# Gated delta rule in a two-layer decoder: whole 128x128 weights at the 32 and 64 levels of the block inverse, and the 64-row inverse turned from its kept transpose

## The chip, the cores and the metric

The kernel runs on one core of one Trainium2 chip. The metric is the device time of one execution in microseconds. Before the change three runs gave 4811.43, 4815.2 and 4816.7 us; the median is 4815.2 us. All work is float32 but for a few masks.

## The reference, cut to what matters

The whole program is two pre-norm decoder layers (attention, cross attention and a mixture of experts in each) on x of shape 8 x 256 x 256. The change touches one of the six parts only, the first part of the second layer:

```python
# x: (8, 256, 256); 16 key heads, DK = 128, values of 2 x 128 for each key head
q = causal_conv_silu(x @ Wq, qcw, qcb);  q = l2norm(q)
k = causal_conv_silu(x @ Wk, kcw, kcb);  k = l2norm(k)
v = causal_conv_silu(x @ Wv, vcw, vcb)
alpha, beta = sigmoid(x @ Wa), sigmoid(x @ Wb)
def step(state, inp):                       # for each of the 256 tokens of a sequence
    qt, kt, vt, at, bt = inp
    state = state * at
    err = vt - einsum('bhkv,bhk->bhv', state, kt)
    state = state + bt * einsum('bhk,bhv->bhkv', kt, err)
    return state, einsum('bhkv,bhk->bhv', state, qt)
out = outs.reshape(b, t, 32 * 128) @ Wo
```

## The kernel before, in words

The recurrence is not run token by token. For one head and one sequence (a *unit*; there are 16 x 8 = 128) the 256 tokens are two blocks of 128. Inside a block the errors solve a triangular system whose matrix is I plus the masked, decayed products of keys; its inverse, multiplied with the values, gives all errors at once. The inverse of a 128x128 block is built in levels. GpSimd inverts the four 32x32 diagonal blocks of each of the two blocks, for eight units at a time (lines 1285 to 1306). TensorE then joins them: at the 32 level two neighbouring inverses of 32 rows give one of 64 rows (`grow_off32`, `grow_t64`), at the 64 level two of 64 rows give the whole one (`grow_off64`, `grow_tt128`). `tt` holds the transpose of the inverse, which the solves need as weights; `t64` holds the upper 64-row inverse not transposed, which the 64 level needs as its moving operand. Before the change `t64` comes from a product of its own in `grow_t64` (line 1416).

The work is a software pipeline. In stage s the unit s is *projected* (8 matmuls with `wkqv`, line 1360), unit s-1 is *prepared* (convolution and silu on VectorE and ScalarE, lengths at 1395, products at 1371, v times Wo at 1385, scaled products into `lp` on VectorE at 1670 and 1673), unit s-16 is *grown* (the levels above) and unit s-17 is *given* (solves at 1447, 1453, 1459, outputs at 1467 to 1471, added to x on VectorE at 1710). There are 145 stages: 16 without a grown unit, 112 with all of them, and a tail of 17. Units alternate between two sets of buffers and PSUM banks (`h` = 0 and 1).

Each engine runs its part of a stage in a fixed written order (the functions named `stage`), and semaphores join them; an engine that comes to a wait holds all that it has behind it. On TensorE the order of a stage is in `stage` below. On ScalarE it is: keep w (1574), scale v (1557), tanh of part 0 (1534), keep tt64 (1564), keep the second w (1574), square (1540), the taps (1526), tanh of part 1, decay (1546), keep tt128 (1569), taps. On VectorE: convolve (1630), keep off32 (1682), convolve, rest (1702), convolve, silu (1640), keep t64 (1690), convolve, keep off64 (1695), keep lengths (1646), silu, add out (1710), scales (1655 to 1660), scale products (1670, 1673), convolve. So the square of the keys, which the lengths on TensorE wait for, stands on ScalarE behind the copy that waits for `solve_second`.

A float32 matmul is two instructions on TensorE (each a weight load and a matmul), so the trace has x4 where the code has two calls; a transpose is one.

Of the kernel before, what the change touches and what calls it, by code (L numbers as in the profile page):

```python
# [25 lines left out]
ALU = mybir.AluOpType  # L26
# [4 lines left out]
P = 128  # L31
B, S, D = 8, 256, 256
# [11 lines left out]
HALF = HD // 2  # L44
# [990 lines left out]
def delta_attention(k):  # L1035


    nc, ins = k.nc, k.ins
# [31 lines left out]
    t_ready = k.sems("dl_t_ready")  # L1070
    t_kept = k.sems("dl_t_kept")
    tt_ready = k.sems("dl_tt_ready")
    tt_kept = k.sems("dl_tt_kept")
# [20 lines left out]
    with ExitStack() as st:  # L1094
        def sb(name, shape, dt=F32):
            return k.sb(f"dl_{name}", shape, dt, st)
# [36 lines left out]
        diag = [sb(f"diag{h}", [P, 2, P]) for h in range(2)]  # L1133
        diag_t = [sb(f"diag_t{h}", [P, 2, HALF]) for h in range(2)]
        off32 = [sb(f"off32{h}", [P, 2, P]) for h in range(2)]
        off64 = [sb(f"off64{h}", [P, 2, HALF]) for h in range(2)]
        t64 = [sb(f"t64{h}", [HALF, 2, HALF]) for h in range(2)]
        tt = [sb(f"tt{h}", [P, 2, P]) for h in range(2)]
        wv = [sb(f"wv{h}", [P, 2, D]) for h in range(2)]
        rest = [sb(f"rest{h}", [P, D]) for h in range(2)]  # L1140
# [1 line left out]
        def bank(h, i, a, b, p0=0, p1=P):  # L1142
            return k.ps[h][p0:p1, i, a:b]

        def blocks(ap):
            return ap.rearrange("p (b s) -> p b s", b=2)
# [17 lines left out]
        with nc.Block() as block:  # L1164
# [93 lines left out]
            def _(pool):  # L1258

                for h in range(2):  # L1260
                    nc.gpsimd.memset(diag[h][:, :, :], 0.0)
                    nc.gpsimd.memset(diag_t[h][:, :, :], 0.0)
                    last = nc.gpsimd.tensor_copy(off32[h][:, :, :], k.ident[:, :].unsqueeze(1).to_broadcast([P, 2, P]))
                last.then_inc(made, 1)
                pool.wait_ge(loaded, 16 * 5)
# [66 lines left out]
            def _(pe):  # L1332
# [20 lines left out]
                def project_part(u, m):  # L1353
                    h = u.h
                    if m == 0:
                        pe.wait_ge(w_loaded[h], u.pair * 16 + 16)

                        wait_past(pe, lp_ready[h], u.count(1))
                    for c in range(DC):
                        last = nc.tensor.matmul(bank(h, m // 2, (m % 2) * S, (m % 2 + 1) * S),  # L1360
                                                wkqv[h][:, c, m * P:(m + 1) * P],
                                                k.xnT[:, c, u.seq * S:(u.seq + 1) * S],
                                                start=c == 0, stop=c == DC - 1)
                    if m % 2:
                        last.then_inc(projected[h], 1)
# [42 lines left out]
                                                diag_t[h][:, blk, :], start=True, stop=True)  # L1408
                    last.then_inc(off_ready[h], 1)

                def grow_t64(u):

                    h = u.h
                    pe.wait_ge(off_kept[h], u.count(2, 1))
                    for blk in range(2):
                        last = nc.tensor.matmul(bank(h, 2, P + blk * HALF, P + (blk + 1) * HALF, 0, HALF), diag[h][0:HALF, blk, 0:HALF],
                                                off32[h][0:HALF, blk, 0:HALF], start=True, stop=True)
                    last.then_inc(t_ready[h], 1)

                    pe.wait_ge(v_scaled[h], min(u.count(1, B), B * HK // 2) if u.fixed else u.count(1, B))  # L1420
                    for blk in range(2):
                        last = nc.tensor.matmul(bank(h, 3, blk * P, (blk + 1) * P), off32[h][:, blk, :],
                                                diag[h][:, blk, :], start=True, stop=True)
                    last.then_inc(tt_ready[h], 1)

                def grow_off64(u):
                    h = u.h
                    pe.wait_ge(t_kept[h], u.count(1, 1))
                    for blk in range(2):
                        last = nc.tensor.matmul(bank(h, 2, blk * HALF, (blk + 1) * HALF, 0, HALF),  # L1430
                                                lp[h][0:HALF, u.seq, blk * S + HALF:blk * S + P],
                                                t64[h][:, blk, :], start=True, stop=True)
                    last.then_inc(off_ready[h], 1)

                def grow_tt128(u):
                    h = u.h
                    pe.wait_ge(off_kept[h], u.count(2, 2))
                    pe.wait_ge(tt_kept[h], u.count(2, 1))
                    for blk in range(2):
                        last = nc.tensor.matmul(bank(h, 2, P + blk * HALF, P + (blk + 1) * HALF, 0, HALF), off64[h][HALF:P, blk, :],  # L1440
                                                tt[h][HALF:P, blk, HALF:P], start=True, stop=True)
                    last.then_inc(tt_ready[h], 1)

                def solve_first(u):
# [29 lines left out]
                def stage(j, s, project, prepared, turned, grown, given):  # L1474
                    if given is not None:
                        solve_first(given)
                    if grown is not None:
                        grow_off32(grown)
                    if project is not None:
                        project_part(project, 0)  # L1480
                    if given is not None:
                        solve_cross(given)
                    if grown is not None:
                        grow_t64(grown)
                    if project is not None:
                        project_part(project, 1)
                    if given is not None:
                        solve_second(given)
                    if project is not None:
                        project_part(project, 2)  # L1490
                    if grown is not None:
                        grow_off64(grown)
                    if prepared is not None:
                        lengths_of(prepared)
                        products_of(prepared, 0)
                    if given is not None:
                        mix(given)
                    if grown is not None:
                        grow_tt128(grown)
                    if project is not None:  # L1500
                        project_part(project, 3)
                    if prepared is not None:
                        products_of(prepared, 1)
                        give_v(prepared)
# [97 lines left out]
            def _(dve):  # L1602
# [84 lines left out]
                def keep_t64(u):  # L1687
                    h = u.h
                    dve.wait_ge(t_ready[h], u.count(1, 1))
                    nc.vector.tensor_copy(t64[h][:, :, :], blocks(bank(h, 2, P, S, 0, HALF))).then_inc(t_kept[h], 1)  # L1690

                def keep_off64(u):
                    h = u.h
                    dve.wait_ge(off_ready[h], u.count(2, 2))
                    nc.vector.tensor_scalar(off64[h][HALF:P, :, :], blocks(bank(h, 2, 0, P, 0, HALF)), -1.0, None, ALU.mult)\
                        .then_inc(off_kept[h], 1)

                def keep_rest(u):
# [574 lines left out]
```

## Time and profile before

| | us |
|---|---|
| median of 3 runs | 4815.2 |
| the profiled execution | 4797.55 |
| its span, first to last instruction | 4795.8 |
| TensorE matmul busy | 3953.1 |
| VectorE busy | 2787.0 |
| ScalarE busy | 1612.8 |
| GpSimd busy | 1345.9 |
| mean granted TensorE clock | 0.92 |

The delta part takes the stretch from about 1560 to 3285 us of the span. Busy shares over the whole span mix six parts; the change must be read from this stretch, and in it from the order of the waits. Start times in a timeline are those of the first instruction of a merged row; busy time of overlapping matmuls is longer than their distance in time, so costs on TensorE are taken as distances between starts.

### The profile page before, as it was taken

How to read it: one execution, taken by the hardware profiler on the slowest of the kernel's cores; microseconds unless marked ns; L12 is line 12 of the kernel's file. 1: busy time of each engine (PE TensorE's matmuls, PEld its weight loads, DVE VectorE, ACT ScalarE, POOL GpSimd, SP SyncE). 2: the span in 40 equal slices, each digit the busy share in tenths (PEclk: the TensorE clock that was granted, in tenths of full speed). 3: DMA queues.
4: the chain of work that ended last, by engine and by line, in shares of the span. 5: the costliest groups of instructions: out<-in, count | busy, mean ns of one | idle time of the engine just before them, and what ended most of it. 6: DMA issues, size and time to landing. Idle time of an engine off the chain costs nothing. (4 is left out here: it accounts for less than half of the span.)

```text
span 4795.8 us, 58977 instructions
## 1 busy us (share of the span) xinstructions
PE 3953.1 (82%) x18543; PEld 2857.4 (60%) x18543; DVE 2787.0 (58%) x7765; ACT 1612.8 (34%) x3960; POOL 1345.9 (28%) x2072
## 2 busy tenths in 40 slices
PE   6999976999997789999999999984899999970230
PEld 4666654555555577777777777762555665550130
DVE  4666654222222778888888888854566666655023
ACT  2444431111111445444454454531344444430010
POOL 0000000000000365545555555550111111115547
PEclk9999986999997999999999999996999999985575
DMA  1000000000000011111111111111000000003240
GB/s 65 0 0 0 0 8 24 12 12 23 11 11 18 20 36 24 39 36 26 36 24 36 31 35 36 23 20 52 1 0 0 0 0 0 0 20 102 52 151 13
DMA packets 198749, 119.39 MB, mean 25 GB/s; under 512 B 122312, under 2 KB 187654, under 8 KB 197520
## 3 DMA queue, kind: packets, MB, share of 16 engines
q1 hardware_dynamic: 181472, 102.85, 8.4%
q0 software_dynamic: 12288, 9.55, 0.7%
q10 hardware_dynamic: 4800, 4.72, 0.3%
q8 instruction: 89, 1.46, 0.1%
q14 instruction: 100, 0.82, 0.1%
HBM read 102.09 MB, written 38.93 MB: 29 GB/s over the span
## 5 line engine op out<-in xcount | busy, mean ns | idle before, releaser
L1630 DVE SCALAR_TENSOR_TENSOR dl_y<-ps,dl_taps,dl_y 128x255 f32<-128x255 f32 (+2 forms) x1536 | 651.5, 473 | 146.9 <-ACT dl_y L1526 142.6
L1360 PE MATMUL ps<-xnT,dl_wkqv 128*128 128x256 f32 x2048 | 549.5, 394 | 29.0 <-DVE dl_lp L1673 22.0
L923 PE MATMUL ps<-xnT,moe_wgu 128*112 x1024 | 447.5, 595 | 5.2 <-DVE moe_ex L963 5.2
L1360 PEld LDWEIGHTS ps<-xnT,dl_wkqv 128*128 128x128 f32 x2048 | 368.0, 193 | 87.5 <-issue 35.4
L362 POOL TENSOR_TENSOR at_rs<-at_ss,mhalf 128x15 f32<-128x15 f32 x32 | 125.5, 3920 | 745.7 <-DVE at_ss L549 745.7
L1283 POOL TENSOR_TENSOR dl_rn<-dl_n,mhalf 128x4 f32<-128x4 f32 x128 | 173.5, 1356 | 568.4 <-DVE dl_n L1646 568.4
L923 PEld LDWEIGHTS ps<-xnT,moe_wgu 128*112 128x112 f32 x1024 | 182.0, 178 | 251.3 <-issue 249.3
L183 POOL TENSOR_TENSOR ln_rstd<-ln_ve,mhalf 128x4 f32<-128x4 f32 x24 | 24.2, 1009 | 1085.5 <-DVE ln_ve L169 1085.5
L448 PE MATMUL ps<-at_shared,at_v 128*128 128x256 f32 (+2 forms) x1280 | 316.4, 380 | 4.6 <-ACT at_shared L672 0.2
L1526 ACT ACTIVATE dl_y<-ps,dl_taps 128x256 f32<-128x256 f32 x512 | 259.7, 559 | 113.6 <-PE ps L1360 113.6
L989 DVE TENSOR_TENSOR moe_hT<-moe_sg,ps 112x1024 f32<-112x1024 f32 x64 | 78.2, 1221 | 372.7 <-ACT moe_sg L947 372.7
L424 PE MATMUL ps<-at_kT,at_qT 128*128 128x320 f32 (+2 forms) x1024 | 271.3, 398 | 2.8 <-ACT at_kT L654 2.8
L1301 POOL TENSOR_TENSOR dl_inv_u<-dl_inv_u,dl_inv_tmp 64x30 f32<-64x30 f32 (+14 forms) x480 | 259.6, 541 | 37.6
L448 PEld LDWEIGHTS ps<-at_shared,at_v 128*128 128x128 f32 (+1 forms) x1280 | 211.5, 191 | 89.6 <-issue 64.3
L947 ACT ACTIVATE moe_sg<-ps 112x1024 f32<-112x1024 f32 x64 | 65.5, 1023 | 571.7 <-PE ps L923 571.7
L438 PE MATMUL ps<-ident,at_probs 128*128 128x128 f32 (+1 forms) x1152 | 173.3, 282 | 96.0 <-DVE at_probs L583 92.7
L456 PE MATMUL ps<-at_wo,at_oT 128*128 (+1 forms) x1024 | 234.8, 382 | 18.6 <-ACT at_oT L677 18.6
L388 PE MATMUL ps<-at_wq,at_xb 128*128 (+1 forms) x512 | 246.3, 615 | 4.5 <-POOL at_xb L356 2.4
L1385 PE MATMUL ps<-dl_wo,dl_z 128*128 128x256 f32 x1024 | 244.9, 383 | 0.0
L1298 POOL TENSOR_TENSOR dl_inv_tmp<-dl_inv_u,dl_inv_a 64x30 f32<-64x30 f32 (+14 forms) x480 | 233.1, 486 | 24.7
L932 PE MATMUL ps<-moe_wd,moe_hT 112*128 112x256 f32 x1024 | 226.3, 379 | 0.0
L438 PEld LDWEIGHTS ps<-ident,at_probs 128*128 128x128 f32 (+1 forms) x1152 | 123.3, 135 | 169.3 <-DVE at_probs L583 156.3
(277 smaller groups left out, 8027.8 us busy)
## 6 DMA issues: line engine op xcount, KB each, us to landing
dl_grow<-decay_rows SPq DMA_DIRECT2D x128, 128.0 KB, 3.0
sp_wgu<-in_w1gu SPq DMA_DIRECT2D x12, 768.0 KB, 10.7
dl_wkqv<-in_w1kqv SPq DMA_DIRECT2D x16, 512.0 KB, 5.2
delta_diag<-dl_lp SPq DMA_DIRECT2D x512, 8.0 KB, 1.5
dl_diag<-delta_diag_tt SPq DMA_DIRECT2D x512, 8.0 KB, 1.7
moe_wgu<-in_w0gu SPq DMA_DIRECT2D x16, 448.0 KB, 3.7
slot_rows<-sp_zero SPq DMA_DIRECT2D x4, 1152.0 KB, 8.1
sp_wd<-in_w1d SPq DMA_DIRECT2D x12, 384.0 KB, 11.3
```

The source lines that it names most:

```text
L388: last = nc.tensor.matmul(k.ps[h][:, t, :], xb[h][:, c, t * P:(t + 1) * P], wq[:, c, ds(group(u) * (G * HD), G * HD)], start=c == 0, stop= ...
L424: last = nc.tensor.matmul(o[:, 0:nk], qT[h][:, r, t * P:(t + 1) * P], kT[h][:, 0:nk], start=True, stop=cross)
L438: last = nc.tensor.transpose(slot(h, (r % 2) * 4 + pieces[j])[0:w, t * P:(t + 1) * P], probs[h][:, (r % 2) * TB + t, j * P:j * P + w], k.i ...
L448: last = nc.tensor.matmul(slot(h, (r % 2) * 4 + 3)[:, c0:S], v[h][0:w, j, :], pT[h][0:w, r % 2, j, c0:S], start=j == 0, stop=j == KT - 1)
L456: last = nc.tensor.matmul(slot(h, t), oT[h][:, hh, t * P:(t + 1) * P], wo[:, ds(group(u) * G + hh, 1), :], start=hh == 0, stop=hh == G - 1)
L923: last = nc.tensor.matmul(k.ps[h][0:IC, m, :], wgu[q][h][:, c, m * IC:(m + 1) * IC], k.xnT[:, c, ds(g * (GT * P), GT * P)], start=c == 0, ...
L1298: nc.gpsimd.tensor_tensor(tmp, inv_u[:, 0:i, i:i + 1].to_broadcast([GP, i, w]), inv_a[:, i:i + 1, i + 1:Q32].to_broadcast([GP, i, w]), ALU ...
L1301: nc.gpsimd.tensor_tensor(inv_u[:, 0:i, i + 1:Q32], inv_u[:, 0:i, i + 1:Q32], tmp, ALU.subtract)\
L1360: last = nc.tensor.matmul(bank(h, m // 2, (m % 2) * S, (m % 2 + 1) * S), wkqv[h][:, c, m * P:(m + 1) * P], k.xnT[:, c, u.seq * S:(u.seq + ...
L1385: last = nc.tensor.matmul(bank(h, 3, t * D, (t + 1) * D), z[h][:, 2 + m, t * P:(t + 1) * P], wo[h][:, m, :], start=m == 0, stop=m == 1)
L1526: last = nc.scalar.activation(y[h][:, m, :], bank(h, m // 2, (m % 2) * S, (m % 2 + 1) * S), ACT.Identity, bias=taps[h][:, m, KC:KC + 1], s ...
L1630: last = nc.vector.scalar_tensor_tensor(y[h][:, m, back:S], bank(h, m // 2, (m % 2) * S, (m % 2 + 1) * S - back), taps[h][:, m, KC - 1 - b ...
```

## The change

Three products work on full 128x128 weights with zeros or the identity in what was left out. `off64` gets a buffer of 128 columns whose rest is zero (a memset on GpSimd ahead of the stages, line 1263 after), `t64` gets 128 rows. `grow_off64` takes all 128 columns of `lp` as weights and so puts its result in rows 64 to 127 of PSUM; `grow_tt128` takes the whole `off64`. The third product, of the 64-row inverse, goes: `grow_t64` becomes `grow_tt64` without it, and a new `turn_tt64` turns the kept `tt` on TensorE (two 128x128 transposes) behind the second projection; it waits for ScalarE's copy of `tt`. In TensorE's stage `lengths_of` moves ahead of `grow_off64`.

```diff
-        off64 = [sb(f"off64{h}", [P, 2, HALF]) for h in range(2)]
-        t64 = [sb(f"t64{h}", [HALF, 2, HALF]) for h in range(2)]
+        off64 = [sb(f"off64{h}", [P, 2, P]) for h in range(2)]
+        t64 = [sb(f"t64{h}", [P, 2, HALF]) for h in range(2)]
...
+                    nc.gpsimd.memset(off64[h][:, :, :], 0.0)
...
-                def grow_t64(u):
+                def grow_tt64(u):
 
                     h = u.h
                     pe.wait_ge(off_kept[h], u.count(2, 1))
-                    for blk in range(2):
-                        last = nc.tensor.matmul(bank(h, 2, P + blk * HALF, P + (blk + 1) * HALF, 0, HALF), diag[h][0:HALF, blk, 0:HALF],
-                                                off32[h][0:HALF, blk, 0:HALF], start=True, stop=True)
-                    last.then_inc(t_ready[h], 1)
...
+                def turn_tt64(u):
+
+                    h = u.h
+                    pe.wait_ge(tt_kept[h], u.count(2, 1))
+                    for blk in range(2):
+                        last = nc.tensor.transpose(bank(h, 2, S + blk * P, S + (blk + 1) * P), tt[h][:, blk, :], k.ident[:, :])
+                    last.then_inc(t_ready[h], 1)
...
                     for blk in range(2):
-                        last = nc.tensor.matmul(bank(h, 2, blk * HALF, (blk + 1) * HALF, 0, HALF),
-                                                lp[h][0:HALF, u.seq, blk * S + HALF:blk * S + P],
+                        last = nc.tensor.matmul(bank(h, 2, blk * HALF, (blk + 1) * HALF), lp[h][:, u.seq, blk * S:blk * S + P],
                                                 t64[h][:, blk, :], start=True, stop=True)
...
-                        last = nc.tensor.matmul(bank(h, 2, P + blk * HALF, P + (blk + 1) * HALF, 0, HALF), off64[h][HALF:P, blk, :],
-                                                tt[h][HALF:P, blk, HALF:P], start=True, stop=True)
+                        last = nc.tensor.matmul(bank(h, 2, P + blk * HALF, P + (blk + 1) * HALF), off64[h][:, blk, :],
+                                                tt[h][:, blk, HALF:P], start=True, stop=True)
...
                     if grown is not None:
-                        grow_t64(grown)
+                        grow_tt64(grown)
                     if project is not None:
                         project_part(project, 1)
+                    if grown is not None:
+                        turn_tt64(grown)
                     if given is not None:
                         solve_second(given)
                     if project is not None:
                         project_part(project, 2)
+                    if prepared is not None:
+                        lengths_of(prepared)
                     if grown is not None:
                         grow_off64(grown)
                     if prepared is not None:
-                        lengths_of(prepared)
                         products_of(prepared, 0)
...
-                    nc.vector.tensor_copy(t64[h][:, :, :], blocks(bank(h, 2, P, S, 0, HALF))).then_inc(t_kept[h], 1)
+                    nc.vector.tensor_copy(t64[h][:, :, :], blocks(bank(h, 2, S, 2 * S))[:, :, 0:HALF]).then_inc(t_kept[h], 1)
...
-                    nc.vector.tensor_scalar(off64[h][HALF:P, :, :], blocks(bank(h, 2, 0, P, 0, HALF)), -1.0, None, ALU.mult)\
+                    nc.vector.tensor_scalar(off64[h][HALF:P, :, 0:HALF], blocks(bank(h, 2, 0, P, HALF, P)), -1.0, None, ALU.mult)\
```

This is TensorE's order from the second solve product (1453) to the first output product (1467) of one full stage, before; the last number is partitions x columns of the result, one row for each code line.

```order
L1453 MATMUL ps<-dl_wv,dl_lp 128x256
L1416 MATMUL ps<-dl_off,dl_diag 64x64 x2
L1422 MATMUL ps<-dl_diag,dl_off 128x128 x2
L1360 MATMUL ps<-xnT,dl_wkqv 128x256 x2
L1459 MATMUL ps<-dl_rest,dl_tt 128x256
L1360 MATMUL ps<-xnT,dl_wkqv 128x256 x2
L1430 MATMUL ps<-dl_t,dl_lp 64x64 x2
L1395 MATMUL ps<-dl_ones,dl_sq 128x1 x4
L1371 MATMUL ps<-dl_z 128x512
L1467 MATMUL ps<-dl_wv,dl_lp 128x256
```

The same stretch of TensorE's order after (the lines moved: 1453 is 1456, 1422 is 1418, 1360 is 1361, 1459 is 1462, 1430 is 1434, 1395 is 1396; the transposes are 1427).

```order
L1456 MATMUL ps<-dl_wv,dl_lp 128x256
L1418 MATMUL ps<-dl_diag,dl_off 128x128 x2
L1361 MATMUL ps<-xnT,dl_wkqv 128x256 x2
L1427 MATMUL ps<-ident,dl_tt 128x128 x2
L1462 MATMUL ps<-dl_rest,dl_tt 128x256
L1361 MATMUL ps<-xnT,dl_wkqv 128x256 x2
L1396 MATMUL ps<-dl_ones,dl_sq 128x1 x4
L1434 MATMUL ps<-dl_t,dl_lp 128x64 x2
L1372 MATMUL ps<-dl_z 128x512
L1470 MATMUL ps<-dl_wv,dl_lp 128x256
```

The product at 1416 is gone, two transposes stand between the second projection and the second solve, and the lengths stand directly behind the third projection, ahead of the 64 level. The orders of ScalarE, VectorE and the DMA queue are the same before and after; GpSimd has the two memsets more.

## Rows read from the trace of the kernel before

**Rows 1.** Full stages: us busy (instructions) of PE, PEld, DVE, ACT, POOL, then clock.

```profile
1762.00:3178.00 1416.00, 1397.25 (x7536) 1115.55 (x7534) 1159.63 (x3102) 704.99 (x1663) 762.91 (x1418) 1.00 0.14 31
```

**Rows 2.** Waits from 1762 to 3178 us: total, times, longest.

```profile
DVE x L1710 <- PE ps L1471: 67.9, 106, 3.1
PEld ps L1416 <- DVE dl_off L1682: 25.4, 57, 0.8
DVE dl_lp L1670 <- PE ps L1371: 8.7, 41, 0.2
```

**Rows 3.** Timeline of TensorE over one full stage: start, length, instructions.

```profile
2506.45 0.59 PE L1471 MATMUL ps<-dl_wv,dl_lp 128*128 128x256 f32 x2
2506.98 0.44 PE L1440 MATMUL ps<-dl_tt,dl_off 64*64 64x64 f32 x4
2507.35 1.13 PE L1360 MATMUL ps<-xnT,dl_wkqv 128*128 128x256 f32 x4
...
2510.91 0.55 PE L1407 MATMUL ps<-dl_diag_t,dl_lp 128*128 128x64 f32 x4
2511.30 1.08 PE L1360 MATMUL ps<-xnT,dl_wkqv 128*128 128x256 f32 x4
2512.22 0.59 PE L1453 MATMUL ps<-dl_wv,dl_lp 128*128 128x256 f32 x2
...
2513.66 1.03 PE L1360 MATMUL ps<-xnT,dl_wkqv 128*128 128x256 f32 x4
2514.53 0.59 PE L1459 MATMUL ps<-dl_rest,dl_tt 128*128 128x256 f32 x2
...
2516.29 1.05 PE L1395 MATMUL ps<-dl_ones,dl_sq 128*128 128x1 f32 x8
...
2519.01 0.38 PE L1471 MATMUL ps<-dl_wv,dl_lp 128*128 128x256 f32 x1
```

**Rows 4.** Timeline of VectorE and ScalarE over the same stage.

```profile
2512.09 0.46 DVE L1682 TENSOR_SCALAR dl_off<-ps 32x64 f32<-32x64 f32 x2
2513.49 0.63 ACT L1534 ACTIVATE dl_z<-dl_y 128x512 f32<-128x512 f32 x1 [1.27 <-DVE dl_y L1630]
2514.03 0.35 ACT L1564 COPY dl_tt<-ps 128x256 f32<-128x256 f32 x1
2515.16 0.37 ACT L1574 COPY dl_wv<-ps 128x256 f32<-128x256 f32 x1 [0.78 <-PE ps L1459]
2515.43 0.63 ACT L1540 ACTIVATE dl_sq<-dl_z 128x512 f32<-128x512 f32 x1
```

**Rows 5.** Timeline of VectorE and TensorE two stages later.

```profile
2531.56 0.59 PE L1471 MATMUL ps<-dl_wv,dl_lp 128*128 128x256 f32 x2
2536.85 0.46 DVE L1682 TENSOR_SCALAR dl_off<-ps 32x64 f32<-32x64 f32 x2
```

**Rows 6.** Timeline of a stage in which VectorE was late.

```profile
2474.57 0.46 DVE L1682 TENSOR_SCALAR dl_off<-ps 32x64 f32<-32x64 f32 x2
2475.08 0.30 PEld L1416 LDWEIGHTS ps<-dl_off,dl_diag 64*64 64x64 f32 x4 [0.83 <-DVE dl_off L1682]
2475.45 0.52 PEld L1422 LDWEIGHTS ps<-dl_diag,dl_off 128*128 128x128 f32 x4
2481.35 0.59 PE L1471 MATMUL ps<-dl_wv,dl_lp 128*128 128x256 f32 x2
```

**Rows 7.** Timeline of TensorE in the first attention: eight transposes.

```profile
562.89 1.09 PE L408 MATMUL ps<-ident,at_t 128*128 128x128 f32 x8 [0.40 <-DVE at_t L536]
```

**Rows 8.** Timeline in the tail, one unit after another.

```profile
3258.99 0.26 ACT L1569 COPY dl_tt<-ps 64x128 f32<-64x128 f32 x1 [2.02 <-PE ps L1440]
3259.30 0.30 PEld L1447 LDWEIGHTS ps<-dl_vs,dl_tt 128*128 128x128 f32 x2 [0.48 <-ACT dl_tt L1569]
3260.43 0.46 DVE L1682 TENSOR_SCALAR dl_off<-ps 32x64 f32<-32x64 f32 x2 [0.93 <-PE ps L1407]
3261.46 0.52 PEld L1422 LDWEIGHTS ps<-dl_diag,dl_off 128*128 128x128 f32 x4
```

## The prediction

> **What bounds the kernel now.** I read the busy time by stretches first, since only the delta part is touched. In the stretch in which every stage has all its units TensorE is busy 1397 of 1416 us at the full clock, VectorE 1160 [rows 1]. That says "TensorE", but two engines work on one unit in turns, and the table of waits shows the other half: VectorE sat 67.9 us until the last output product (1471), and TensorE's weight load at 1416 was released by VectorE's off32 copy in 57 of 111 stages [rows 2]. So I read one stage as a loop with two anchors. A is the first of the two instructions of line 1471, K the end of VectorE's copy at 1682.
>
> In the stage shown A is at 2506.45 and the next A at 2519.01, a period of 12.56 us [rows 3]. K is 2512.09 + 0.46 = 2512.55 [rows 4], so A to K takes 6.10 and K to the next A 6.46 us. Two stages on, A is 2531.56 and K 2537.31 [rows 5]: A to K takes 5.75, and TensorE, which has kept its period, is what comes late there. From A to K VectorE works without a pause but for the wait at 1710, so this half is VectorE's; a shorter TensorE leaves it as it is. Where VectorE itself is late, K is 2475.03, the weight load follows at 2475.08 and the next A at 2481.35: 6.32 us is TensorE's shortest K to A [rows 6]. Both loops, TensorE's own and the one through VectorE, stand within a few tenths of each other, and I price both.
>
> **The change on TensorE alone.** Each 64-row product is entered and left at a price. The two instructions of 1471 should take 0.43 us (0.87 for the four of 1360, 2513.66 to 2514.53), but 1440 starts 0.53 after them: 0.10 to get in. Its four instructions hold the engine 0.37, and the first instruction behind it is longer than elsewhere (1.13 against 1.03 for the four of 1360), since its weights could not be loaded ahead: 0.10 to get out. That is 0.57 us for each of three products, 1.71 in a stage [rows 3].
>
> The Trainium skill says under TensorEngine Tiling (Array Packing), Key Properties, that changing the tiling mode drains the engine; the trace agrees, with 0.10 us on the way in and 0.10 out. It speaks for the change. The page TensorE: Matmul & The Clock Gate, LDWEIGHTS, speaks against it: a weight load costs by its columns, so 128 in place of 64 cost twice. The rows agree with that too: four loads of 64 columns span 0.30, four of 128 span 0.52 us [rows 6]. By that rule alone the change would add 3 x 0.22 us a stage less what the third product becomes; the sum below has both effects in it, since it takes distances between starts.
>
> In their place come: `grow_off64` and `grow_tt128` with whole weights and 64 columns, the very form of 1407, which holds the engine 0.39 (2510.91 to 2511.30) plus 0.05 by which the next block is longer (0.92 from 2511.30 to 2512.22 against 0.87), so 0.44 each [rows 3]; and two transposes, of which eight take 1.09 us, at most 0.14 each and about 0.12 [rows 7], so 0.23. The sum is 1.71 - 0.88 - 0.23 = 0.60 us less of TensorE, a period of 11.96 if nothing else were in the way.
>
> **The loop through VectorE.** Here the two edits of the order count. I follow one stage from K, all times after K. VectorE's convolution, then ScalarE's tanh, then the copy of tt64 behind it on ScalarE: that copy starts at 2514.03 and ends at 2514.38, K + 1.83 [rows 4]. Nothing of this waits for TensorE, so it stays, however early the product of tt64 is. Before, nobody needed `tt` for a long time. Now `turn_tt64` does, at the head of TensorE's queue. TensorE gets there sooner: the product can start at about K + 0.16 (0.05 from a release to the weight load, as 3259.25 to 3259.30 [rows 8], and 0.11 for the load), then 0.44 and 0.87 of the projection, so at K + 1.47. It stands until K + 1.83 + 0.05, the first transpose runs at 1.99, and the second solve product (1459 before) at 1.99 + 0.23 = K + 2.22. Before, it ran at 2514.53, K + 1.98. Instead of gaining, it is 0.24 late. Queued behind the waiting transpose is all of TensorE's stage.
>
> On ScalarE the copy of w waits for that product, and the square of the keys stands behind it: it ends at 2515.43 + 0.63 = 2516.06, 1.53 behind the product [rows 3, 4]. So now it ends at K + 3.75, and the weight load of the lengths goes at K + 3.80. TensorE is there earlier: the third projection ends at 2.22 + 0.43 + 0.87 = 3.52. Before, `grow_off64` stood in this gap and covered it; now it has been moved behind. So the lengths start at K + 3.80 in place of 3.74 (2516.29). From there to A took 2.72 (2516.29 to 2519.01) and now has `grow_off64` in it, 0.44 more. K to A is 3.80 + 2.72 + 0.44 = 6.96 us, against 6.46 in this stage.
>
> `grow_off64` itself waits for nothing: the transposes end near K + 2.4, VectorE copies t64 by K + 2.8, and the product comes at about 4.7. The copies at 1690 and 1695 keep 128 elements a partition; I price them as unchanged. Silu, taps, the copy of off64 and the inverse lengths move by at most 0.3 us and have VectorE's wait at 1710 as cover; if that cover went, the same 0.3 would come on top.
>
> A to K: 5.75 and 6.10 are the ends seen. The stages of a group of eight lie between them, nearer to the shorter, and I take 5.90. The period is then 5.90 + 6.96 = 12.86, 0.30 more than 12.56; with the ends 12.71 and 13.06, so 0.15 to 0.50 more. Once in eight stages VectorE is held by GpSimd's inverse lengths, and the K to A of that stage grows from 6.32 to 6.96; the stage before it has used up 0.30 of the hold, so it costs 0.34 too. 112 stages x 0.30 = 34 us. VectorE waited 41 times for the second key product at 1371 [rows 2]; that now comes 0.13 sooner (0.57 - 0.44, for `grow_tt128`): 5 us back.
>
> **The tail.** In the last 17 stages only the growing and the solves are left, and the chain runs bare. Without the 64-row product the weights of tt64 can go 0.05 after off32 is kept at 3260.89, so at 3260.94 in place of 3261.46: 0.52 less [rows 8]. From that load to the load of the second solve there were 0.44. Now it is 0.11 + 0.33 to the last product's start, 0.28 until it is out, 0.04 + 0.35 for ScalarE's copy, 0.05 and 0.23 for the transposes: 1.39, or 0.95 more. With 0.07 at the second level's end this is 0.5 us for each of 16 units, 8 us. The two memsets lie ahead of the stages; even at a microsecond together they are not seen.
>
> **Sum.** 34 - 5 + 8 = +37 us on the profiled execution of 4797.6 (span 4795.8), 4835. The median of the runs shown is 4815.2, 0.37% above it; against that the same +37 gives 4852 us.
>
> **The rivals.**
> First, TensorE's own stream decides, and the change is faster. The place is the stretch of full stages, the price 0.60 us in 112 stages, -67 us, and with the tail 4815 - 67 + 8 = 4756. TensorE's 1397 of 1416 us speak for it, and the skill's rule on the mode switch, cited above, with a drain of 0.20 us each time. It decides only if both waits vanish: tt64 kept before K + 1.4, and the square done before K + 3.0. Then K to A is 0.16 + 0.44 + 0.87 + 0.23 + 0.43 + 0.87 to the lengths, 2.61 from there and 0.44 for `grow_off64`, 6.05, and with 5.90 the period is 11.95. Against it: the copy ends at K + 1.83 in the stage shown, the tanh ahead of it being held by VectorE, and without this wait the square would still end 1.53 behind the second solve.
> Second, the two waits are half as long as I work out, since ScalarE and VectorE shift against each other with the new phase. The period stays at 12.56 plus at most 0.05; the tail's 8 us remain: 4815 to 4825, say 4818.
> Third, the shift against GpSimd makes A to K the longer 6.10 in most stages, as the inverse runs beside it in six of eight. Then it is 0.50 x 112 = 56, + 8 = 4879. A lower clock in the thinner tail would add to it: at 1.2 GHz in place of 2.4 its products take twice as long, a few us.
> Fourth, the change doesn't do what it says: then no 64-row products would vanish from the trace. The order of instructions rules it out.
>
> **How the numbers follow.** Forecast 0.66, first rival 0.11, second 0.10, third 0.13. The range runs from 4812, which takes in the second rival, to 4885, which takes in the third; the first, 0.11, and some mishap beyond 4885 stay out. I call 0.2%, about 10 us, what a measurement of this kernel tells from no change. Faster by more than that: 0.12; within it: 0.10; slower: 0.78.
>
> **What would show it.** Period between two A: 12.8 to 12.9, where 11.96 would prove the first rival. No 64x64 matmul left, and the sum of TensorE's gaps grown from near 0 to 0.3 to 0.5 us ahead of the transposes, released by ScalarE's copy at 1564, and 0.2 to 0.4 ahead of the lengths, released by the square. The second solve at K + 2.2, the next A at K + 7.0. The tail's units 6.5 apart. If the first transposes find `tt` kept, or if A to K shrinks below 5.5, my sum is wrong.

## The result and the profile after

The changed kernel is slower: 4822.51 us median (4812.02 to 4829.03, 16 runs) against 4808.4 us of the kernel before in as many runs (4803.82 to 4816.7). The medians differ by 14 us; the ratio is 1.0025, 95% interval 1.0018 to 1.0033, which is +12 us. The prediction had +37. The sign was right, the size about three times too large. (The prediction stood on a median of three runs, 4815.2, which is 7 us above that of the 16; its 4852 was off by this too.)

The profiled execution of after has a span of 4820.2 us, that of before 4795.8, but not all of these 24 us are the change's. On TensorE the delta part starts 3 us earlier in the trace of after and ends 6 us later, so it is 8 us longer. The other 18 to 19 us came behind it, most of them between about 4320 and 4610 us of the span, in the last of the six parts, which has the same instructions in both kernels. From the last A to the end of the span after took 1531 us; in the other nine traces of this document it is 1513 to 1518. The execution profiled before took 4797.55 us, 11 less than the median of its 16 and less than the fastest of them; that of after, 4822.06, is at its median. So what the change does is read from its stages below, and not from the spans.

Busy time in the full stages, as [rows 1] (columns: stretch, length, then PE, PEld, DVE, ACT and POOL busy with instructions, granted clock, DMA share, GB/s):

```profile
1762.00:3178.00 1416.00, 1374.70 (x7257) 1132.87 (x7256) 1134.18 (x3082) 693.11 (x1649) 759.15 (x1410) 1.00 0.14 31
```

TensorE has become less busy, 1375 of 1416 us where it was 1397, and its weight loads (PEld) busier, 1133 where they took 1116. It does less and waits more. The waits of the same kernel, from 1770 to 3150 us (total, times, longest):

```profile
DVE x L1716 <- PE ps L1474: 90.8, 105, 0.9
PEld ps L1396 <- ACT dl_sq L1546: 56.7, 107, 0.5
PEld ps L1427 <- ACT dl_tt L1570: 46.4, 102, 0.6
PEld ps L1418 <- DVE dl_off L1688: 10.8, 13, 0.8
```

The two waits that were forecast are there in nearly every stage: the weight load of the lengths for the square, 0.53 us each, and that of the transposes for the copy of tt64, 0.45 each. Neither stood in the table of before. TensorE's wait for off32, there in 57 of 111 stages [rows 2], is left in 13.

The timeline of one full stage of after, from one A (the first instruction of 1474, which was 1471) to the next; rows in between are left out:

```profile
2424.76 0.59 PE L1474 MATMUL ps<-dl_wv,dl_lp 128*128 128x256 f32 x2
2426.50 0.59 PE L1372 MATMUL ps<-dl_z 128*128 128x256 f32 x2
2427.19 0.75 DVE L1676 SCALAR_TENSOR_TENSOR dl_lp<-ps,dl_cj,dl_dec 128x512 f32<-128x512 f32 x1 [0.15 <-PE ps L1372]
2429.92 0.46 DVE L1688 TENSOR_SCALAR dl_off<-ps 32x64 f32<-32x64 f32 x2
2430.62 0.63 PEld L1418 LDWEIGHTS ps<-dl_diag,dl_off 128*128 128x128 f32 x4
2431.85 0.35 ACT L1570 COPY dl_tt<-ps 128x256 f32<-128x256 f32 x1
2432.26 0.20 PEld L1427 LDWEIGHTS ps<-ident,dl_tt 128*128 128x128 f32 x2 [0.36 <-ACT dl_tt L1570]
2432.54 0.60 PE L1462 MATMUL ps<-dl_rest,dl_tt 128*128 128x256 f32 x2
2433.44 0.63 ACT L1546 ACTIVATE dl_sq<-dl_z 128x512 f32<-128x512 f32 x1
2434.12 0.97 PEld L1396 LDWEIGHTS ps<-dl_ones,dl_sq 128*128 128x128 f32 x8 [0.53 <-ACT dl_sq L1546]
2435.04 0.64 PE L1434 MATMUL ps<-dl_t,dl_lp 128*128 128x64 f32 x4
2437.29 0.59 PE L1474 MATMUL ps<-dl_wv,dl_lp 128*128 128x256 f32 x2
```

K (the end of 1688) is 2430.38. From K the copy of tt64 ends at 1.82, the second solve (1462) runs at 2.16, the square ends at 3.69, the load of the lengths goes at 3.74 and the next A is at 6.91. The forecast had 1.83, 2.22, 3.75, 3.80 and 6.96. So K to A came out within 0.05 us, and it is 6.91 in nearly every stage of the trace, whatever A to K was: the loop through VectorE and ScalarE decides nearly all of them. In before the period was 12.55 whether A to K took 5.75 or 6.10, so there it was TensorE's own stream that decided. The other half, A to K, is 5.62 here. The forecast had 5.90.

The tail of the changed kernel, one unit, from one A to the next, in the timeline of TensorE:

```profile
3244.26 0.59 PE L1474 MATMUL ps<-dl_wv,dl_lp 128*128 128x256 f32 x2
3248.41 0.20 PEld L1427 LDWEIGHTS ps<-ident,dl_tt 128*128 128x128 f32 x2 [0.65 <-ACT dl_tt L1570]
3250.71 0.59 PE L1474 MATMUL ps<-dl_wv,dl_lp 128*128 128x256 f32 x2
```

(Rows in between are left out.) A unit takes 6.45 us (3250.71 - 3244.26); before it took 6.05, start of A to start of A. Of the difference, the wait of the transposes for the copy of tt64, 0.65 us, is what the reader is to see here; it has no row in the tail before [rows 8].

Taken together, from the starts of A in both traces (110 periods of full stages, then the tail). A *held* stage is the first of each group of eight, in which VectorE is held up by GpSimd's inverse:

| us | before | after |
|---|---|---|
| first A to the 111th | 1405.0 | 1414.2 |
| period in the 96 other stages, mean | 12.60 | 12.63 |
| of it A to K | 5.89 | 5.69 |
| of it K to A | 6.70 | 6.94 |
| period in the 14 held stages, mean | 13.98 | 14.38 |
| last full stage, 111th to 112th A | 12.93 | 14.21 |
| tail, 112th to last A | 112.0 | 115.8 |

From the first A to the last this is 14.3 us more. The warm-up ahead of the first A took 5 us less in after (221 against 227 from the delta part's first instruction on TensorE). The change touches only the last two stages of this stretch, and it takes 221 to 231 us in the ten traces, so I don't count it to the change.

Some single stages are long for a reason that the stages themselves don't show: the clock that TensorE was granted. In after the 105th stage took 16.46 us, and the clock was at half (1.2 GHz in place of 2.4) for 3.4 us of it; the same holds for the last full stage (14.21 us, 3.4 at half; before 12.93 us, 2.3 at half). These two stages are 4.1 us longer than the same two in before.

### The profile page after: what moved, and what is told of

Its sections match the earlier page's. It is cut to its first block and busy times, and to the rows that moved or that the text cites. A ratio compares the mean times of both kernels' runs of the same rounds, so it can differ in the third digit from the quotient of the medians.

```text
span 4820.2 us, 58595 instructions
## 1 busy us (share of the span) xinstructions
PE 3937.6 (82%) x18287; PEld 2890.7 (60%) x18287; DVE 2775.0 (58%) x7765; ACT 1607.8 (33%) x3960; POOL 1350.1 (28%) x2074
```

## The experiments

The two theories throughout: the loop A to K to A with its waits sets the time; or the rival, that whole weights cost TensorE more load time than the drains gave back. Ratios are against the kernel before, run on the same chip, 95% interval behind them. Stages are counted within a group of eight; the first is the held one.

**The lengths back behind the 64-level product.** In the changed kernel:

```diff
-                    if prepared is not None:
-                        lengths_of(prepared)
                     if grown is not None:
                         grow_off64(grown)
                     if prepared is not None:
+                        lengths_of(prepared)
                         products_of(prepared, 0)
```

> The changed kernel with one edit undone: the lengths stand behind the 64-level product again. Theory (the loop of waits A to K to A sets the time): the product of 0.44 us stands in the gap in which the lengths wait for the square, so K to A falls from 6.91 to 6.50 us. A to K grows back in the three stages of eight in which GpSimd's inverse collides with the small VectorE operations (5.62 to 5.85 becomes 5.95 to 6.10), since the inverse lengths come 0.26 us later relative to A. Mean period of a full stage near 12.3 in place of 12.6; ratio to the kernel before 0.994 to 0.997. Rival (the whole weights cost TensorE more than the drains gave back): the same products are there, so the time stays at that of the changed kernel, ratio 1.0025.

Measured: 0.9988 (0.9980 to 0.9997), 4793.2 us beside 4798.1. K to A is 6.51 as expected, and the wait for the square is gone from the table. A to K is 6.02 and 6.25 in stages 2 to 4 of a group of eight and 5.62 in the last three, so the periods are 12.53, 12.77, 12.75, 12.49 and three of 12.13. The mean of the stages that aren't held, 12.45, is above the 12.3 expected, and so the gain on before is smaller, 0.1% where 0.3 to 0.6% were expected (the estimate had left the stages 2 to 4 at 5.95 to 6.10). The rival's 1.0025 is excluded: the same products, at 0.37% less than the changed kernel.

**The copy of tt64 ahead of the tanh.** In the changed kernel, on ScalarE:

```diff
-                    if prepared is not None:
-                        tanh_of(prepared, 0)
                     if grown is not None:
                         keep_tt64(grown)
+                    if prepared is not None:
+                        tanh_of(prepared, 0)
```

> The changed kernel with one edit: ScalarE copies tt64 ahead of the tanh of part 0. Theory: the copy no longer stands behind VectorE's convolution, tt is kept at K + 1.2 and the transposes wait for nothing; the second solve comes at K + 1.7 to 1.9 in place of 2.15, K to A becomes 6.45 to 6.6 in place of 6.91, the period about 12.25. The wait ahead of the lengths stays (0.3 to 0.4 us a stage). Ratio to before 0.992 to 0.996. Rival (load time of whole weights): no change from the changed kernel, 1.0025.

Measured: 0.998 (0.9971 to 0.9988), 4788.7 us beside 4798.1. The wait ahead of the transposes is gone, the one ahead of the lengths stays (66.2 us in 110 stages). The period is 12.36 in six of eight stages, 0.1 more than expected, and the expectation's loop is not what sets it: it is 12.36 whether A to K takes 5.62 or 5.84, and K to A is then 6.74 or 6.52. What decides is a second loop, which does not pass through K: second solve, copy of w, square, lengths, and TensorE's stream from there to the next second solve. It is TensorE's own stream, 11.96, with 0.29 of waiting for the square in it and 0.10 more in the blocks behind the lengths. (The stage behind a held one is 12.66, since there the square starts 0.30 us later: it waits for VectorE's silu (1646), which is late from the hold.) A miss in size: 0.2% gained where 0.4 to 0.8% were expected; in the trace the tail also costs 4.8 us more than in before.

**Both edits together.**

> The changed kernel with both edits: lengths behind the 64-level product and the copy of tt64 ahead of the tanh. Theory: both waits vanish and TensorE's own stream decides, 11.96 us in most full stages, about 12.15 in the two where GpSimd holds VectorE; mean 12.0. 112 stages times 0.55 is 62 us and more below before: ratio 0.985 to 0.989. Rival: no change from the changed kernel.

Measured: 0.9909 (0.9895 to 0.9923), 4755.9 us beside 4798.1. This is faster than both kernels. The waits of this kernel, from 1770 to 3150 us:

```profile
PEld ps L1418 <- DVE dl_off L1687: 26.5, 60, 0.8
PEld ps L1427 <- ACT dl_tt L1569: 3.3, 5, 0.7
```

And its timeline over one stage:

```profile
2384.33 0.59 PE L1474 MATMUL ps<-dl_wv,dl_lp 128*128 128x256 f32 x2
2384.76 0.55 PE L1443 MATMUL ps<-dl_tt,dl_off 128*128 128x64 f32 x4
2385.15 1.08 PE L1361 MATMUL ps<-xnT,dl_wkqv 128*128 128x256 f32 x4
...
2390.62 0.52 PEld L1418 LDWEIGHTS ps<-dl_diag,dl_off 128*128 128x128 f32 x4 [0.45 <-DVE dl_off L1687]
...
2392.03 0.38 PE L1427 MATMUL ps<-ident,dl_tt 128*128 128x128 f32 x2
2392.25 0.60 PE L1462 MATMUL ps<-dl_rest,dl_tt 128*128 128x256 f32 x2
2392.68 1.03 PE L1361 MATMUL ps<-xnT,dl_wkqv 128*128 128x256 f32 x4
2393.55 0.55 PE L1434 MATMUL ps<-dl_t,dl_lp 128*128 128x64 f32 x4
2393.94 1.00 PE L1396 MATMUL ps<-dl_ones,dl_sq 128*128 128x1 f32 x8
2394.80 1.10 PE L1372 MATMUL ps<-dl_z 128*128 128x512 f32 x2
...
2396.61 0.59 PE L1474 MATMUL ps<-dl_wv,dl_lp 128*128 128x256 f32 x2
```

From the transposes to the next A one block follows the other without a wait. This stage has 12.28, since VectorE was late (A to K is 6.23) and the load at 1418 waited for its off32; K to A is 6.05 here, the figure that the prediction gave under its first rival. Four of eight stages have 11.96, the figure that it worked out for TensorE's own stream (12.56 - 1.71 + 0.88 + 0.23). So the cost of a 64-row product and of its replacements was right, and the first rival was right about TensorE and failed by the two waits alone. The total is 0.9% and not the 1.1 to 1.5% expected: the held stages stay near 14.1 us whatever TensorE does, and the tail costs its 0.40 a unit.

**Whole weights at three places, no turn, lengths where they were.** In the changed kernel, `t64` from a product with 128x128 weights (the cut leaves out that VectorE copies it from the product's place in PSUM, and that the lengths go back behind `grow_off64`):

```diff
                     pe.wait_ge(off_kept[h], u.count(2, 1))
+                    for blk in range(2):
+                        last = nc.tensor.matmul(bank(h, 2, P + blk * HALF, P + (blk + 1) * HALF), diag[h][:, blk, :],
+                                                off32[h][:, blk, 0:HALF], start=True, stop=True)
+                    last.then_inc(t_ready[h], 1)
...
-                    if grown is not None:
-                        turn_tt64(grown)
```

> Whole weights at all three places but no turn: t64 comes from a product of its own with 128x128 weights (0.44 us), right at the off32 copy, and the lengths stand where they stood before. Theory: no wait for ScalarE's copy is added and no 64-row product is left; TensorE's stream is 12.55 - 1.71 + 3 x 0.44 = 12.16 us a stage and decides. Ratio to before 0.989 to 0.993, faster than before although it has the most weight loads of all. Rival (load time of whole weights): it has 4 loads of 128 columns more than the changed kernel less the transposes, so it is slower than the changed kernel, ratio 1.006 or more.

Measured: 0.9956 (0.9941 to 0.9971), 4777.2 us beside 4798.1. The period is 12.19 in the last three stages of a group (12.16 expected; the seventh is longer in every second group) and 12.25 to 12.53 in stages 2 to 5, where GpSimd holds VectorE. It is faster than before and than the changed kernel with the most weight load time of all (1169 us of 1380, where before has 1089 and the changed kernel 1106), so load time is out as the cause. It gained about half of what was expected.

This trace has single stages of 15.2, 15.9, 16.2 and 17.7 us. In the last three of them the granted clock fell to half, for 3.4, 3.4 and 6.8 us. The last row is the busy time of the engines in a stretch, with the granted clock, 0.50, as the third number from its end. The longest, with A at 2352.31:

```profile
2358.93 1.10 PE L1361 MATMUL ps<-xnT,dl_wkqv 128*128 128x256 f32 x4 [1.73 <-DVE dl_lp L1680]
2362.76 1.91 PE L1361 MATMUL ps<-xnT,dl_wkqv 128*128 128x256 f32 x4
2364.46 1.06 PE L1466 MATMUL ps<-dl_rest,dl_tt 128*128 128x256 f32 x2
2362.00:2366.00 4.00, 4.00 (x13) 3.37 (x13) 2.58 (x7) 1.21 (x4) 0.97 (x2) 0.50 0.18 43
```

TensorE had waited 1.73 us for VectorE in this held stage, and the clock was at half from 2360.08 on, for 6.8 us: the four products at 2362.76 hold the engine 1.70 us in place of 0.87. In the other two it had waited 2.16 us for VectorE and 1.85 us for the transfer of the projection's weights just before. Not every such wait is followed by it: the kernel with both edits has one of 2.09 us at full clock.

**Before with the lengths moved.** Only the move of `lengths_of` of the diff, on the kernel before.

> The kernel before with one edit: the lengths ahead of the 64-level product. Theory (loop A to K to A): the lengths now wait for the square, which ends 1.53 us behind the second solve, and TensorE has nothing to do meanwhile: 0.39 us of wait in each full stage, period 12.94, ratio to before 1.006 to 1.010. The inverse lengths on GpSimd come 0.57 us earlier relative to A, so the small VectorE operations at 1655 to 1660 collide less with the elimination: A to K falls in the stages that had 5.97 to 6.10, towards 5.75 to 5.85. Rival (A to K is VectorE's alone, as the prediction had it): A to K keeps 5.75 to 6.10. Rival (weight loads decide): nothing is added, so the time stays at 1.000.

Measured: 1.0058 (1.0044 to 1.0072), 4825.4 us beside 4796.4. This one edit costs 28 us, more than the whole change. The wait for the square is in the table in place of nothing before:

```profile
PEld ps L1395 <- ACT dl_sq L1541: 57.3, 106, 0.6
```

The period is 12.84 in all seven stages that aren't held (12.94 expected: 0.29 lost and not 0.39; the lengths start 1.58 us behind the second solve, and solve and third projection take 1.30 of it, so the wait is 0.28; the estimate was higher by 0.11, which is what it gave the weight load elsewhere). It is 12.84 whatever A to K is, so here too the loop through the square decides and not the one through K. A to K is 5.75 in five of them and 5.82 in two, where before had 5.97, 6.10 and 6.10. The rival that A to K is VectorE's alone falls here: nothing was taken from VectorE.

**Before with the 128-row product alone on whole weights.** The memset, the wide `off64` and:

```diff
-                        last = nc.tensor.matmul(bank(h, 2, P + blk * HALF, P + (blk + 1) * HALF, 0, HALF), off64[h][HALF:P, blk, :],
-                                                tt[h][HALF:P, blk, HALF:P], start=True, stop=True)
+                        last = nc.tensor.matmul(bank(h, 2, P + blk * HALF, P + (blk + 1) * HALF), off64[h][:, blk, :],
+                                                tt[h][:, blk, HALF:P], start=True, stop=True)
```

> The kernel before with the 128-row product (1440) alone on whole weights, nothing moved. Theory: one 64-row product of 0.57 us becomes one of 0.44, behind A and ahead of the second key product (1371), so that ends 0.13 us sooner after A. In the stages in which VectorE waited for it A to K falls from 5.75 to 5.62; in those with 5.97 to 6.10 it stays, since GpSimd holds VectorE there. TensorE's stream is 12.55 - 0.13 = 12.42, ratio 0.996 to 0.998. Rival (weight loads decide): slower, 1.002 to 1.005.

Measured: 0.9973 (0.9962 to 0.9984), 4784.6 us beside 4796.4. The period is 12.43 in all stages that aren't held (12.42 expected), but for the seventh of some groups. A to K is 5.62 in the last three of a group, where it was 5.75, and 5.97, 6.12, 6.11, 5.85 in the others, as before. So the 0.13 us of the shorter product reach K in full, but only where GpSimd does not hold VectorE.

**No elimination on GpSimd, after and before.** Both kernels without the calls of `eliminate`:

```diff
-    STEPS = 2 + 2 * (Q32 - 2)
+    STEPS = 2
...
-                    for i in range(CUTS[part], CUTS[part + 1]):
-                        eliminate(g, i)
```

> The changed kernel with GpSimd's elimination steps (the two operations of each step) left out, so the 32-row inverses are not computed. Theory (VectorE's small operations are slowed by GpSimd's elimination beside them): A to K becomes 5.62 in all stages of a group, where it was 5.85 in two of eight, and the period 12.53 in all; the held stage of each group falls from 14.2 to about 12.5 to 13. K to A stays at 6.91, since nothing of it is GpSimd's. Rival (A to K varies for another reason, by position or buffers): 5.85 and 12.76 remain in those two stages.

> The kernel before with GpSimd's elimination steps left out, so the 32-row inverses are not computed. Theory: A to K is 5.75 in every stage in place of 5.75 to 6.10, now always set by the second key product; the period stays 12.55, since TensorE's stream decides. Rival: A to K keeps 5.97 to 6.10 in the first three stages of a group.

Measured, one run each and so without an interval: 4778.7 us (after) and 4779.1 (before), beside 4796.4. A to K is 5.62 in seven of eight stages of the changed kernel, but for a few first stages of a group, with K to A at 6.91 and a period of 12.53. In the kernel before it is 5.75 in the same seven, again but for a few first stages, with 12.55, except for the seventh stage of every second group, which has about 13.5: there TensorE waits up to 1.2 us for the transfer of the projection's weights. The held stage has moved, not gone: it is now the sixth of a group, with 13.5 after and 13.2 before. There GpSimd's last copy of a group (1307, 1.97 us) runs behind the inverse lengths, and VectorE's operation on two columns beside it (1659) takes 0.90 us and ends within 0.02 us of it. So the spread of A to K from 5.62 to 5.85, and from 5.75 to 6.10, is the elimination's.

How it does so is in the timelines; rows in between are left out. First the kernel before in the third stage of a group, A at 2392.26:

```profile
2393.79 0.64 POOL L1301 TENSOR_TENSOR dl_inv_u<-dl_inv_u,dl_inv_tmp 64x238 f32<-64x238 f32 x1
2393.90 0.55 DVE L1655 SCALAR_TENSOR_TENSOR dl_nk<-dl_n,dl_rn 128x2 f32<-128x2 f32 x1
2394.51 0.61 POOL L1298 TENSOR_TENSOR dl_inv_tmp<-dl_inv_u,dl_inv_a 64x240 f32<-64x240 f32 x1
2394.63 0.51 DVE L1660 TENSOR_TENSOR dl_cj<-dl_cj,dl_rn 128x2 f32<-128x2 f32 x1
2395.17 0.75 DVE L1670 SCALAR_TENSOR_TENSOR dl_lp<-ps,dl_cj,dl_dec 128x512 f32<-128x512 f32 x1
```

The same stage after, A at 2386.72:

```profile
2388.00 0.64 POOL L1302 TENSOR_TENSOR dl_inv_u<-dl_inv_u,dl_inv_tmp 64x238 f32<-64x238 f32 x1
2388.37 0.28 DVE L1661 SCALAR_TENSOR_TENSOR dl_nk<-dl_n,dl_rn 128x2 f32<-128x2 f32 x1
2388.72 0.61 POOL L1299 TENSOR_TENSOR dl_inv_tmp<-dl_inv_u,dl_inv_a 64x240 f32<-64x240 f32 x1
2388.83 0.51 DVE L1666 TENSOR_TENSOR dl_cj<-dl_cj,dl_rn 128x2 f32<-128x2 f32 x1
2389.38 0.75 DVE L1676 SCALAR_TENSOR_TENSOR dl_lp<-ps,dl_cj,dl_dec 128x512 f32<-128x512 f32 x1
```

And without the elimination:

```profile
2383.11 0.16 DVE L1659 SCALAR_TENSOR_TENSOR dl_nk<-dl_n,dl_rn 128x2 f32<-128x2 f32 x1
2383.45 0.16 DVE L1664 TENSOR_TENSOR dl_cj<-dl_cj,dl_rn 128x2 f32<-128x2 f32 x1
2383.89 0.75 DVE L1674 SCALAR_TENSOR_TENSOR dl_lp<-ps,dl_cj,dl_dec 128x512 f32<-128x512 f32 x1 [0.28 <-PE ps L1370]
```

An operation on two columns takes 0.16 us alone and 0.55 beside GpSimd, and it ends when GpSimd's ends: 2393.79 + 0.64 = 2394.43 against 2393.90 + 0.55 = 2394.45, and 2395.12 against 2395.14. In the 110 stages of before 1655 was held 70 times and 1660 84 times (0.25 us and more), and each time the end lies within 0.03 us of the end of a GpSimd operation. The scaled product at 1670 takes 0.75 in all three, and in all 110, the 84 with a GpSimd operation beside it included. GpSimd's chain starts with the inverse lengths, and these follow the lengths on TensorE. After the change the lengths stand further ahead of A, so the whole row of GpSimd operations lies 0.25 us earlier behind A (1.28 in place of 1.53), and VectorE's held operation is let go 0.25 sooner.

The Trainium skill, SBUF — State Buffer, section Who interferes with whom, says that a VectorE instruction with two SBUF inputs contends with a GpSimd instruction that reads SBUF, and it calls the ports that the two share an exclusive lock. The trace agrees to 0.03 us: 1655 and 1660, which read two tiles of SBUF, wait for the end of GpSimd's operation; 1670, with one input in PSUM, does not. Two inputs are not the whole story in this trace: 1656, a copy of one tile, took up to 0.32 us in place of 0.16 in 40 of the 110 stages, also to the end of a GpSimd operation, and 1658, which reads two tiles, took 0.15 in all 110.

How far do single traces bear out the totals? The stretch from the first A to the last, less that of before (1530.0 us), beside the measured difference (the ratio less 1, times before's median; for the last two the one run less that median), in us:

| kernel | first to last A | measured |
|---|---|---|
| the changed kernel | +14.3 | +12 |
| lengths back | -6.6 | -6 |
| copy first | -8.4 | -10 |
| both | -46.3 | -44 |
| whole product | -14.0 | -21 |
| lengths moved, on before | +28.4 | +28 |
| 128-row product alone, on before | -5.7 | -13 |
| before without the elimination | -18.0 | -17 |
| after without the elimination | -16.5 | -18 |

Seven agree within 3 us. The traces of the other two have one held stage each of 17.7 and 17.9 us, with the clock at half for 6.8 us, some 4 us over the other held stages; the rest of their difference is not explained. So the delta part carries the totals, to a few us.

## Why the prediction was wrong in size

The step that failed is the size of one term, A to K: the prediction held it at 5.90 us, and it measured 5.69. The terms, as the prediction put them:

- TensorE's stream, 0.60 us less in a stage, 11.96: right, shown by the kernel with both edits. One reading beside it was loose: four loads of 64 columns span 0.30 us and four of 128 span 0.52, which is 1.7 times and not twice; the sum did not use it.
- The wait at `turn_tt64`, second solve at K + 2.22: right, 2.16. The wait of the lengths, load at K + 3.80: right, 3.74. K to A 6.96: right, 6.91. These two waits are why the change is not faster; each taken away alone gives a kernel faster than before, if by 0.1 to 0.2% only, since the other one stays.
- "This half is VectorE's; a shorter TensorE leaves it as it is", A to K 5.90: wrong, and this is the step that failed. 5.90 was right for before (5.89), but it is 5.69 after, over the stages that aren't held. Two things in it are TensorE's. The second key product is 0.13 us nearer to A, since the 128-row product is shorter; and it is what the scaled product waits for as soon as GpSimd is out of the way. And the lengths on TensorE time GpSimd's operations, which hold the small ones on VectorE; they moved by 0.25 us. The shorter product alone gave 5.62 in three stages of seven, the moved lengths alone 5.75 to 5.82 in the first three.
- "5 us back" for the 41 waits at 1371: the same mistake, taken from the table of waits. That table counts idle time (41 times, 0.2 us each), not in how many stages the product was what came last.
- The base of 12.56: the stages that aren't held had 12.60 in the mean, with their irregular ones: the seventh of every second group took 12.83 to 14.27 us, and in four of them TensorE is seen to wait for the transfer of the projection's weights, up to 1.51 us. With 5.69 in place of 5.90 the prediction's own sum gives 12.65, and 12.63 was measured: 0.03 us a stage more than before and not 0.30. That is 3 us in these 96 stages and not 29.
- The held stage, 0.34 more: 0.40 in the mean (13.98 to 14.38), 14 times, about 6 of the 9 us in the full stages. It is right as far as this can tell: the held stages scatter from 13.57 to 14.80 before, 0.2 of the 0.40 is the one stage of 16.46 us with its clock at half, and without it the mean grows by 0.21, the median of all by 0.48.
- The tail, 0.5 a unit and 8 us: 0.40 a unit, but 3.8 us in all. Units that run ahead of a transfer only wait less for it: the long period, in which TensorE waits for the transfer of the last diagonal inverses (8.5 us before, 3.6 after), fell from 17.2 to 12.5 us, while one ahead of it grew from 7.2 to 11.6, 6.7 us of it with the clock at half. Without the elimination, where there is no such wait, the tail costs 5.0 us more (100.3 to 105.3).

The second rival came nearest in time ("the period stays at 12.56 plus at most 0.05"), but for another reason: both waits have the size that I worked out, and the other half of the loop paid for them. The third was wrong about the direction: the shift against GpSimd made A to K shorter, not longer. Of the signs, the second solve, the next A and the tail's 6.5 came as written, the period of 12.8 to 12.9 did not: it is 12.53 in five of seven stages and 12.76 in two. The one that was to give the error away, A to K below 5.5, was set too low; 5.62 was enough.

That the time lies inside the range from 4812 to 4885 is partly luck: the range reached down to 4812 for the second rival's sake, and the forecast's own ends, 0.15 and 0.50 a stage, both lie far above the 0.03 measured.

What stays open: why some of TensorE's long waits are followed by a lower clock and others are not, and what made the last part of the program 13 to 18 us longer in the one trace of after.

## What to carry to other kernels

Where two engines work in turns, price both halves of the loop, and ask of the half that looks like one engine's what else times it: there the operand that comes last, and the neighbour engine whose operation must end first. When a wait is taken away, look for the next loop: here the one through the square, 12.36 us, stood close behind the one through K, 12.53. Moving work off the front of a wait uncovers the wait: the product that was moved behind the lengths had covered 0.3 us of it, and one change of order alone cost 0.58%. A copy that nobody waited for may stand anywhere on its engine; when a change makes it needed, move it as well.

## What the runs showed of the hardware

A 64-row product (two 64x64 blocks, four instructions) between whole ones costs 0.57 us [rows 3]: 0.10 to get in, 0.37 in it, 0.10 behind it. With whole weights it costs 0.44, although it loads twice the columns; one such exchange took the period from 12.55 to 12.43. A float32 transpose of 128x128 is one instruction and takes 0.11 us in a stream, a product of the same size two. A VectorE operation on two columns can take 0.55 us in place of 0.16, to the end of the GpSimd operation beside it. And in three stages of one kernel, after waits of 1.7 to 2.2 us, TensorE was granted half its clock for 3.4 to 6.8 us, in which its products took twice as long.
